# Last layer of a small conditioned transformer: first batch through all four experts first, grouped rows added to the result by indirect transfers

## The chip, the cores and the metric

The kernel runs on one core of a Trainium2 chip (trn2). The metric is device time in microseconds of one execution, median over runs. A profile is one further execution, recorded by the hardware profiler; its times are counted from the start of its span.

## The reference

The input is `x` of shape (4, 512, 288), four batches of 512 tokens, and a condition vector for each batch. A rotation of a 64-dimensional subspace comes first, then three transformer layers (attention with 16 heads, then a multilayer perceptron, each with shift, scale and gate from the condition). Only the last layer's perceptron matters here. It is a mixture of four experts with the best two chosen for each token:

```python
xn = _modulate(_ln(x), sh_mlp, sc_mlp)
xf = xn.reshape(-1, C)
gate_logits = xf @ w_gate
topk_logits, topk_idx = jax.lax.top_k(gate_logits, TOP_K)      # TOP_K = 2
gates = jax.nn.softmax(topk_logits, axis=-1)
cw = jnp.sum(jax.nn.one_hot(topk_idx, NUM_EXPERTS) * gates[..., None], axis=1)
hmid = gelu(jnp.einsum('tc,ech->eth', xf, w1) + b1[:, None, :])   # C = 288, hidden 1152
eo = jnp.einsum('eth,ehc->etc', hmid, w2) + b2[:, None, :]
moe = jnp.einsum('te,etc->tc', cw, eo).reshape(B, N, C)
return x + g_mlp[:, None, :] * moe
```

## The kernel before

Everything is written out by hand over ticks. Each engine walks through the same list of ticks, `TICKS`, and does at each of them its share of the main loop and then its items of the agenda (`items`, `agenda`, with a lag per kind and engine in `LAG`). The engines are in order, and only semaphores hold them together: a tick is a place in each engine's program, not a time.

A perceptron pass (a window) takes 512 token rows through one expert: nine hidden tiles of 128, two ticks each, 18 ticks. At an even tick TensorE multiplies a hidden tile (`hidden`, seven matmuls in split precision), at an odd one the back product of the tile two before it (`back`, twelve matmuls). ScalarE applies the gelu (`gelu_tile`); VectorE splits its result in a high and a low half (`G`), two operations. Weights come in six pieces per pass (`load_piece` on the SP queue), ScalarE takes the high half and, in the last layer, VectorE the low half (kind `split`). At the end of a pass VectorE adds the bias from PSUM into `rowt` (`finish`, kind `fin`, at tick 4 of the next pass).

The last layer has 13 passes. Batch 0 goes through each expert with all its rows; the rows of batches 1 to 3 are grouped by expert, in nine tiles of 512 rows. The order before is: batch 0 by experts 0, 1, 2 (`FRONT = 3`), the nine grouped tiles, and batch 0 by expert 3. Beside the first three passes the grouping is made for each batch: norm (`stats2`, `mean2` with GpSimd's `norm`), transposes (`ln2`: ScalarE takes the high part, GpSimd the low part), gate matmul (`gate`), logits turned (`gturn`; VectorE's `choose`), power on GpSimd (`gexp`), places within each expert (`rank`), weights (`weigh`), and modulated rows (`mod`, into the buffers `XG`). GpSimd then writes the rows to their places in the DRAM tensor `tok_rows` (`scatter`: eight indirect transfers, one for each quarter of the tokens and each of the two experts; it waits until they have landed). `table` works out which expert and which rows each tile has, `slots` where each token's two results will stand.

For a grouped tile SP loads its rows (`xg`, `tile_load`), TensorE transposes them in three parts (`lng`) with ScalarE's high and GpSimd's low parts, and after the pass SP stores `rowt` to the DRAM tensor `exp_rows` (`store`). In the last pass GpSimd gathers each token's two results (24 indirect transfers, `gather`); VectorE weighs and adds them, multiplies by the batch's gate and adds to the residual `X` (`merge`), and SP writes the four batches of the output.

Of the kernel before, what the change touches and what calls it, by code (L numbers as in the profile page):

```python
# [46 lines left out]
FRONT = 3  # L47
# [4 lines left out]
CW = C + 64  # L52
FAR = 65536.0
PLACED = 16 * 8
CONSTS = 32
# [171 lines left out]
def expert_of(v):  # L227

    return v if v < FRONT else v - GROUPED


def grouped_window(l, v):

    out = [(4, "fin", l, v - 1, 0)] if v > 0 else []
    i = v - FRONT
    if v > 0 and tile_of(v - 1) is not None:
        out += [(5, "store", l, i - 1, 0)]
    if v == 0:
        out += leaving(l) + [(4, "modrow", l, 1, 0), (12, "mod", l, 1, 0)]
        out += [(14, "gate", l, 0, 0), (15, "gturn", l, 0, 0), (16, "gexp", l, 0, 0), (18, "weigh", l, 0, 0)]  # L240
        out += [(16, "gate", l, 1, 0), (18, "gturn", l, 1, 0), (20, "gexp", l, 1, 0), (21, "rank", l, 1, 0), (23, "weigh", l, 1, 0)]
        out += [(22, "scatter", l, 1, 0)]
    if v == 1:
        out += [(t // 2, "stats2", l, 2, t) for t in range(TT)] + [(2, "mean2", l, 2, 0), (0, "modrow", l, 2, 0)]
        out += [(8 + c, "ln2", l, 2, c) for c in range(3)] + [(8, "mod", l, 2, 0)]
        out += [(11, "gate", l, 2, 0), (13, "gturn", l, 2, 0), (15, "gexp", l, 2, 0), (16, "rank", l, 2, 0), (18, "weigh", l, 2, 0)]
        out += [(17, "scatter", l, 2, 0)]
        out += [(9 + t // 2, "stats2", l, 3, t) for t in range(TT)] + [(11, "mean2", l, 3, 0), (11, "modrow", l, 3, 0)]
        out += [(15 + c, "ln2", l, 3, c) for c in range(3)] + [(17, "mod", l, 3, 0)]
    if v == 2:  # L250
        out += [(0, "gate", l, 3, 0), (2, "gturn", l, 3, 0), (4, "gexp", l, 3, 0), (5, "rank", l, 3, 0), (7, "weigh", l, 3, 0)]
        out += [(6, "scatter", l, 3, 0), (6, "table", l, 0, 0), (10, "slots", l, 0, 0)]
    if v + 1 < WINDOWS[l]:
        first = PIECE["w1", l, v + 1, 0]
        loads = {0: (-2, -2, 4, 6, 9, 11), 1: (0, 1, 2, 8, 10, 12), 2: (-3, -2, -1, 8, 10, 11)}.get(v, (-3, -2, -1, 8, 10, 12))
        out += [(t, "load", l, first + q, 0) for q, t in enumerate(loads)]
        out += [(t, "split", l, first + q, 0) for q, t in enumerate((5, 7, 9, 12, 14, 16) if v > 0 else (1, 3, 7, 9, 12, 15))]
        out += [(9 if v > 0 else 16, "side", l, v + 1, 0)]
    if i == -1:
        out += [(12, "xg", l, 0, 0)] + [(15 + c, "lng", l, 0, c) for c in range(3)]  # L260
    if 0 <= i < GROUPED - 1:
        out += [(1, "xg", l, i + 1, 0)] + [(11 + 2 * c, "lng", l, i + 1, c) for c in range(3)]
# [75 lines left out]
def row_room(l, s, i):  # L338
# [12 lines left out]
                gturn=0, weigh=0, rank=0, table=0, slots=0, merge=0, mod=0, split=1),  # L351
    "POOL": dict(gexp=0, setup=0, scatter=0, gather=0, mean1=1, mean2=1, ln1=1, ln2=1, lng=1, qk=1, out=1, proj=1, tok=1, root=3, split=1, centre=1, fin=1, wg=1,
                 ones=0, vones=0),
    "SP": dict(onerow=0, qk=2, max=1, place=0, load=0, wp=0, agate=0, mlpc=0, b2=0,
               modrow=0, xg=0, store=0, side=0),
# [32 lines left out]
def build(nc, a, out):  # L388
    with ExitStack() as ctx:  # L389
# [11 lines left out]
        tok_rows = nc.dram_tensor("tok_rows", (XROWS, CW), F32).ap()  # L401
        exp_rows = nc.dram_tensor("exp_rows", (GROUPED * N, C), F32).ap()
# [24 lines left out]

        XG = [at(o_qk + 43776 + 5632 * z, f"XG{z}", [128, TT, CW]) for z in range(2)]
        modr = at(o_qk + 43776 + 11264, "modr", [128, 2, CW])

        GA = [[XG[r][:, :, 0:C] for r in range(2)]]
        GA += [[at(o + 4608 * r, f"GA{o}{r}", [128, TT, C])[:, :, :] for r in range(2)] for o in (o_qk, o_qk + 23040)]

# [28 lines left out]
        X = rest("X", [128, B * TT, C])  # L462
        ident = rest("ident", [128, 128])
# [7 lines left out]
        euler = rest("euler", [128, TT, 4])  # L471
        xn = rest("xn", [128, TT, C + 64])
# [26 lines left out]
        cw = at(o_squares + 544, "cw", [128, B, TT, 4])  # L499
        idx = at(o_squares + 800, "idx", [128, SEL, TT, 2], U32)  # L500
        yidx = at(o_squares + 896, "yidx", [128, SEL, TT, 2], U32)
        cws = at(o_squares + 992, "cws", [128, SEL, TT, 2])
# [13 lines left out]
        moved = rest("moved", [128, 4])  # L516
# [5 lines left out]

        slot_a, slot_b = (rowt[:, k, 0:4 * SEL * TT].rearrange("p (n e) -> p n e", e=4) for k in range(2))
        slot_lohi = rowt[:, 2, 0:2 * SEL * TT].rearrange("p (n r) -> p n r", r=2)
# [176 lines left out]
        slots_ready = sem("slots_ready")  # L701
        yg_in = [sem(f"yg_in{j}") for j in range(SEL)]
        merged = sem("merged")
# [75 lines left out]
        def _(sp):  # L779
# [72 lines left out]
            for l in range(LAYERS):  # L852
# [6 lines left out]
            sp.dma_start(tok_rows.rearrange("(k p) c -> p k c", p=128),  # L859
                         act32[:, 0, 0:CW].unsqueeze(1).broadcast_to([128, XROWS // 128, CW])).then_inc(zero_out, 16)  # L860
# [11 lines left out]
            sp.wait_ge(zero_out, 16)  # L872
# [111 lines left out]
            for todo in agenda("SP"):  # L984
                for kind, l, i, k in todo:
# [14 lines left out]
                    elif kind == "store":  # L1000
                        tile_store(l, i)
# [4 lines left out]
            for b in (1, 0, 2, 3):  # L1006
                if b > 0:
                    sp.wait_ge(merged, b)
                else:
                    sp.wait_ge(out_ready, TT)  # L1010
                sp.dma_start(out[b].rearrange("(t p) c -> p t c", p=128), X[:, TT * b:TT * b + TT, :]).then_inc(out_done, 16)
            sp.wait_ge(out_done, 16 * B)

        @block.gpsimd
        def _(pool):
# [92 lines left out]
            def work(kind, l, i, k):  # L1108
# [79 lines left out]
                elif kind == "scatter":  # L1188

                    pool.wait_ge(zero_out, 16)  # L1190
                    pool.wait_ge(mod_done, i)
                    pool.wait_ge(idx_ready, i)
                    for t in range(TT):
# [4 lines left out]
                elif kind == "gather":  # L1198
                    if i == 0:
                        pool.wait_ge(ys_out, 16 * GROUPED)  # L1200
                        pool.wait_ge(slots_ready, 1)
                        pool.wait_ge(misc_full, MISC["lng", l, GROUPED - 1, 2] + 1)

                        pool.wait_ge(acc_full, TT * (WBASE[l] + FRONT + GROUPED))
                    for t in range(TT):
                        for r in range(2):
                            pool.indirect_dma_start(GA[i][r][:, t, :], None, exp_rows,
                                                    bass.IndirectOffsetOnAxis(yidx[:, i, t, r:r + 1], 0)).then_inc(yg_in[i], 16)
                    if i == SEL - 1:
                        for j in range(SEL):  # L1210
                            pool.wait_ge(yg_in[j], 16 * 2 * TT)
# [31 lines left out]
        def _(dve):  # L1243
# [138 lines left out]
            def finish(l, v):  # L1382
# [7 lines left out]
                if l == LAST and v > FRONT:  # L1390
                    dve.wait_ge(ys_out, 16 * min(v - FRONT, GROUPED))
# [3 lines left out]
                if l < LAST or tile_of(v) is not None:  # L1395
# [6 lines left out]
                for t in range(TT):  # L1402
                    ins = dve.scalar_tensor_tensor(out=X[:, TT * b + t, :], in0=rowt[:, t, :], scalar=cw[:, b, t, e:e + 1],  # L1403
# [8 lines left out]
            def merge(j, part):  # L1412

                first, second = GA[j]
                if part == 0:
                    dve.wait_ge(yg_in[j], 16 * 2 * TT)
                    for t in range(TT):
                        dve.tensor_scalar(first[:, t, :], first[:, t, :], cws[:, j, t, 0:1], None, ALU.mult).then_inc(dve_done, 1)  # L1418
                        step()
                    dve.wait_ge(dve_done, steps[0])  # L1420
                    for t in range(TT):
                        dve.scalar_tensor_tensor(out=first[:, t, :], in0=second[:, t, :], scalar=cws[:, j, t, 1:2],  # L1422
                                                 in1=first[:, t, :], op0=ALU.mult, op1=ALU.add).then_inc(dve_done, 1)
                        step()
                    return
                xb = X[:, TT * (j + 1):TT * (j + 2), :]
                dve.wait_ge(dve_done, steps[0])
                dve.wait_ge(mlp_in, mlp_in_total(LAST))
# [995 lines left out]
```

## Time and profile before

| | us |
|---|---|
| median of 3 runs | 1889.64 |
| lowest, highest | 1887.38, 1892.05 |
| the profiled execution, its own time | 1903.3 |
| its span | 1901.6 |

TensorE is busy for 88% of the span (1682.3 us), VectorE for 63%, ScalarE for 51%, GpSimd for 33%. The mean granted TensorE clock is 0.935 of full speed. The profile's page has for each engine its busy time, its share of the span and its number of instructions; then the span in 40 slices, the transfers, the chain that ended last and the costliest groups of instructions. The last layer's perceptron begins around 1398 us.

### The profile page before, as it was taken

How to read it: one execution, taken by the hardware profiler on the slowest of the kernel's cores; microseconds unless marked ns; L12 is line 12 of the kernel's file. 1: busy time of each engine (PE TensorE's matmuls, PEld its weight loads, DVE VectorE, ACT ScalarE, POOL GpSimd, SP SyncE). 2: the span in 40 equal slices, each digit the busy share in tenths (PEclk: the TensorE clock that was granted, in tenths of full speed). 3: DMA queues.
4: the chain of work that ended last, by engine and by line, in shares of the span. 5: the costliest groups of instructions: out<-in, count | busy, mean ns of one | idle time of the engine just before them, and what ended most of it. 6: DMA issues, size and time to landing. Idle time of an engine off the chain costs nothing. (4 is left out here: it accounts for less than half of the span.)

```text
span 1901.6 us, 27789 instructions
## 1 busy us (share of the span) xinstructions
PE 1682.3 (88%) x9395; PEld 1075.8 (57%) x9395; DVE 1196.0 (63%) x2624; ACT 978.7 (51%) x1720; POOL 629.8 (33%) x641
## 2 busy tenths in 40 slices
PE   6776899989998989899899999999898679999993
PEld 2443444433796634344369764444356469999992
DVE  7863677763565767677436567777548376656555
ACT  2323476657354466676655337676664235454530
POOL 4432122214554423341445332231435431111113
PEclk9999799989998879899889989999889799999996
DMA  7712333231001322313200213323223144544423
GB/s 247 246 61 65 103 103 93 93 108 48 11 1 42 101 72 70 92 55 114 70 20 1 88 54 102 101 91 98 72 70 118 65 127 125 156 138 155 140 82 106
DMA packets 104381, 175.98 MB, mean 93 GB/s; under 512 B 13675, under 2 KB 58659, under 8 KB 103951
## 3 DMA queue, kind: packets, MB, share of 16 engines
q1 hardware_dynamic: 101552, 166.33, 28.4%
q0 software_dynamic: 2688, 7.87, 1.3%
q8 instruction: 76, 1.25, 0.3%
q14 instruction: 65, 0.53, 0.1%
HBM read 122.48 MB, written 51.19 MB: 91 GB/s over the span
## 5 line engine op out<-in xcount | busy, mean ns | idle before, releaser
L1379 DVE TENSOR_REDUCE negmax<-ps 128x1 f32<-128x512 f32 x768 | 487.9, 680 | 233.1 <-PE ps L2152 229.7
L1978 ACT ACTIVATE Pr<-ps 128x512 f32<-128x512 f32 x768 | 410.9, 602 | 221.0 <-PE ps L2170 220.7
L1991 ACT ACTIVATE g<-ps,b1col 128x512 f32<-128x512 f32 x189 | 129.8, 688 | 301.9 <-PE ps L2131 247.9
L2170 PE MATMUL ps<-QK 55*128 55x512 f32 x768 | 240.5, 518 | 37.4 <-ACT Pr L1978 26.4
L2216 PE MATMUL ps<-W2a,G 128*128 128x288 f32 x1620 | 246.7, 302 | 13.0 <-issue 10.0
L2216 PEld LDWEIGHTS ps<-W2a,G 128*128 128x128 f32 x1620 | 231.6, 191 | 27.4 <-issue 13.7
L2184 PE MATMUL ps<-Pr,V 128*32 128x512 f32 x1536 | 224.9, 660 | 0.0
L2152 PE MATMUL ps<-QK 54*128 54x512 f32 x768 | 195.9, 445 | 23.6 <-DVE negmax L1379 7.9
L2170 PEld LDWEIGHTS ps<-QK 55*128 55x128 f32 x768 | 92.5, 193 | 204.6 <-ACT Pr L1978 106.9
L1733 DVE CAST G<-g 128x512 fp32r<-128x512 f32 x189 | 103.0, 545 | 157.3 <-ACT g L1991 152.2
L1134 POOL TENSOR_TENSOR HQ<-act,HQ 128x512 fp32r<-128x512 f32 (+1 forms) x69 | 91.6, 1327 | 254.3 <-ACT HQ L1953 120.1
L1735 DVE TENSOR_TENSOR G<-g,G 128x512 fp32r<-128x512 f32 x189 | 149.1, 789 | 6.5
L1134 POOL TENSOR_TENSOR stage<-act,stage 126x512 fp32r<-126x512 f32 (+1 forms) x60 | 77.4, 1289 | 205.7 <-ACT stage L1970 168.1
L2131 PE MATMUL ps<-HQ,W1a 128*128 128x512 f32 x441 | 121.5, 416 | 11.0 <-ACT g L1991 11.0
L2294 PE MATMUL ps<-WP,oT 128*128 128x288 f32 x384 | 126.3, 461 | 2.3 <-DVE oT L1650 2.2
L2152 PEld LDWEIGHTS ps<-QK 54*128 54x128 f32 x768 | 95.8, 199 | 49.2 <-DVE negmax L1379 23.0
L2294 PEld LDWEIGHTS ps<-WP,oT 128*128 128x128 f32 x384 | 72.8, 207 | 69.5 <-issue 35.6
L2131 PE MATMUL ps<-WQ,HQ 128*128 128x288 f32 (+1 forms) x560 | 99.2, 319 | 8.0 <-ACT stage L1970 3.3
L2131 PEld LDWEIGHTS ps<-WQ,HQ 128*128 128x128 f32 (+1 forms) x560 | 81.4, 198 | 43.2 <-issue 14.6
L2131 PE MATMUL ps<-HQ,W1b 128*128 128x512 f32 (+1 forms) x378 | 100.1, 404 | 2.7 <-POOL HQ L1134 2.7
L1139 POOL TENSOR_TENSOR oTok<-oTok,rsum 128x512 f32<-128x512 f32 x48 | 51.2, 1066 | 152.5 <-DVE rsum L1644 151.5
L2131 PEld LDWEIGHTS ps<-HQ,W1a 128*128 128x128 f32 x441 | 82.4, 196 | 31.7 <-ACT g L1991 14.4
(285 smaller groups left out, 2462.8 us busy)
## 6 DMA issues: line engine op xcount, KB each, us to landing
QK<-heads_t SPq DMA_DIRECT2D x192, 144.0 KB
heads_t<-stage SPq DMA_DIRECT2D x96, 252.0 KB
raw<-in_w SPq DMA_DIRECT2D x30, 576.0 KB
raw<-in_w SPq DMA_DIRECT2D x34, 432.0 KB
QK<-heads_t SPq DMA_DIRECT2D x192, 72.0 KB
tok_rows<-act SPq DMA_DIRECT2D x1, 10560.0 KB, 34.4
XG<-tok_rows SPq DMA_DIRECT2D x9, 704.0 KB, 4.3
WA<-in_ada_w SPq DMA_DIRECT2D x3, 1728.0 KB
```

Source lines behind the costliest of these rows:

```text
L1134: pool.tensor_tensor(lo, act32[rows, h % 2, :], hi.bitcast(F32), ALU.subtract).then_inc(low_done, 1)
L1379: dve.tensor_reduce(negmax[:, m % 2, h, t:t + 1], ps[:, row_bank(l, s, i), :], AX, ALU.max, negate=True).then_inc(a_free, 1)
L1733: dve.tensor_copy(G[:, n % 3, 0, :], g32[:, n % 2, :]).then_inc(g_hi, 1)
L1735: dve.tensor_tensor(G[:, n % 3, 1, :], g32[:, n % 2, :], G[:, n % 3, 0, :].bitcast(F32), ALU.subtract).then_inc(g_lo, 1)
L1978: act.activation(Pr[:, t % 2, 2 * half + pair, :], ps[:, (16 * s + u) % 3, :], ACT.Exp, scale=SCALE).then_inc(b_free, 1)
L1991: act.activation(g32[:, n % 2, :], ps[:, hidden_bank(s), :], ACT.Gelu if l == 1 else ACT.Gelu_apprx_tanh, bias=b1col[:, v % 4 if l == LAST ...
L2131: ins = mm(o, lhs(w, h, rows[w]), rhs(w, h, rows[w]), start=p == 0, stop=p == 6)
L2152: mm(ps[:, row_bank(l, s, i), :], QK[r:r + QROW, g, 0, pair, 128 * t:128 * t + 128], QK[r:r + QROW, g, 1, pair, :], start=True, stop=True) ...
L2170: mm(ps[:, k % 3, :], QK[r:r + QROW + 1, g, 1, pair, 128 * t:128 * t + 128], QK[r:r + QROW + 1, g, 0, pair, :], start=True, stop=True).the ...
L2184: ins = mm(ps[32 * i:32 * i + 32, 6, :], V[:, s // 4 % 2, t, c:c + 32], Pr[:, t % 2, i, :], start=t == 0, stop=t == TT - 1)
L2216: ins = mm(ps[:, t, 0:C], G[:, n % 3, x, 128 * t:128 * t + 128], W2[w_ % 2][:, w, ft, :], start=ft == 0 and p == 0, stop=ft == FT - 1 and ...
L2294: ins = mm(bank[:, 0:C], oT[:, (STEPS * l + 4 * i + g) % 5, 128 * k:128 * k + 128], WP[:, g, :], start=g == 0, stop=g == 3)
```

## The change

Batch 0 goes through all four experts first (`FRONT = 4`); the nine grouped tiles come behind. The grouping is spread over the first three passes and one load into the fourth, with later ticks for most items. The last pass is a grouped tile.

A row in `tok_rows` becomes longer by eight values (`PAY = CW + 8`): its four expert weights (written by `weigh`), three values that mark its batch (written by `mod`), and its row number in the output. Rows never written hold zero weights and the number of a row of batch 0, laid down when the buffer is filled at the start, in four transfers now.

For each grouped tile VectorE reads these values (`extras`, kind `ext`): the row numbers as integers, the weight of the tile's expert, and weight times batch mark. It makes from them the tile's gate, four times one product and two multiply-adds (`gates`, kind `gsum`), and after the pass it multiplies `rowt` by it into one of two buffers. GpSimd adds these rows to the output in DRAM by four indirect transfers with addition (`yadd`, at tick 4 of the next pass), and waits until they have landed. The output rows of batches 1 to 3 without the perceptron's part, and later batch 0's, are written beforehand (`init`). Stores to `exp_rows`, `slots`, `gather` and `merge` go.

```diff
-FRONT = 3
+FRONT = EXPERTS[-1]
+PAY = CW + 8
@@ def grouped_window(l, v): @@
-        out += [(5, "store", l, i - 1, 0)]
+        out += [(4, "yadd", l, i - 1, 0)]
     if v == 0:
-        out += leaving(l) + [(4, "modrow", l, 1, 0), (12, "mod", l, 1, 0)]
...
+        out += leaving(l)
+        for b, gate, turn, power, place, weight, move in ((0, 14, 15, 16, None, 18, None), (1, 17, 19, 21, 22, 23, 30),
+                                                          (2, 30, 32, 35, 35, 37, 42), (3, 43, 45, 47, 48, 50, 51)):
+            out += [(gate, "gate", l, b, 0), (turn, "gturn", l, b, 0), (power, "gexp", l, b, 0), (weight, "weigh", l, b, 0)]
+            if b > 0:
+                out += [(place, "rank", l, b, 0), (move, "scatter", l, b, 0)]
+        out += [(4, "modrow", l, 1, 0), (12, "mod", l, 1, 0), (18, "modrow", l, 2, 0), (29, "mod", l, 2, 0),
+                (31, "modrow", l, 3, 0), (38, "mod", l, 3, 0), (50, "table", l, 0, 0)]
+        out += [(16 + t // 2, "stats2", l, 2, t) for t in range(TT)] + [(18, "mean2", l, 2, 0)]
+        out += [(24 + 2 * c, "ln2", l, 2, c) for c in range(3)]
+        out += [(26 + t // 2, "stats2", l, 3, t) for t in range(TT)] + [(28, "mean2", l, 3, 0)]
+        out += [(36 + 2 * c, "ln2", l, 3, c) for c in range(3)]
+        out += [(17, "init", l, b, 0) for b in range(1, B)]
...
-        out += [(12, "xg", l, 0, 0)] + [(15 + c, "lng", l, 0, c) for c in range(3)]
+        out += [(4, "xg", l, 0, 0), (14, "ext", l, 0, 0)] + [(11 + 2 * c, "lng", l, 0, c) for c in range(3)]
+    if i == 0:
+        out += [(6, "init", l, 0, 0)]
...
+    if i >= 0:
+        out += [(6 + 2 * t, "gsum", l, i, t) for t in range(TT)]
     if v == WINDOWS[l] - 1:
-        out += [(6, "gather", l, j, 0) for j in range(SEL)]
-        out += [(t, "merge", l, j, part) for j, t in ((0, 16), (1, 20), (2, 21)) for part in range(2)]
-        out += [(21, "fin", l, v, 0)]
+        out += [(21, "fin", l, v, 0), (21, "yadd", l, i, 0)]
@@ gpsimd @@
+                elif kind == "yadd":
...
+                    pool.wait_ge(ext_ready, i + 1)
                     for t in range(TT):
+                        pool.wait_ge(res_ready, TT * i + t + 1)
+                        pool.indirect_dma_start(out_rows, bass.IndirectOffsetOnAxis(ids[:, i % 2, t:t + 1], 0),
+                                                res[i % 2][:, t, :], None, compute_op=ALU.add).then_inc(ys_out, 16)
+                    pool.wait_ge(ys_out, 16 * TT * (i + 1))
@@ vector, finish @@
+                if l == LAST and v >= FRONT:
+                    i = v - FRONT
+                    if i >= 2:
+                        dve.wait_ge(ys_out, 16 * TT * (i - 1))
+                    for t in range(TT):
+                        dve.wait_ge(acc_free, TT * U + t + 1)
+                        dve.tensor_tensor(res[i % 2][:, t, :], rowt[:, t, :], gsum[:, t, :], ALU.mult).then_inc(res_ready, 1)
+                    return
@@ vector @@
+            def gates(l, i, t):
...
+                dve.tensor_scalar(gsum[:, t, :], gbc[:, 1, :], wgt[:, i % 2, t, 0:1], None, ALU.mult).then_inc(dve_done, 1)
                 dve.wait_ge(dve_done, step())
+                for j in range(1, SEL):
+                    dve.scalar_tensor_tensor(out=gsum[:, t, :], in0=gbc[:, j + 1, :], scalar=wgt[:, i % 2, t, j:j + 1],
+                                             in1=gsum[:, t, :], op0=ALU.mult, op1=ALU.add).then_inc(dve_done, 1)
+                    dve.wait_ge(dve_done, step())
```

## Rows read from the trace of the kernel before

**Rows 1.** Windows: length, busy us (x instructions) of each engine, granted clock, DMA share.

```profile
1441.44:1497.66 56.22, 42.68 (x229) 35.55 (x227) 36.85 (x124) 24.47 (x36) 27.41 (x23) 0.85 0.35 109
1497.66:1560.04 62.38, 39.22 (x208) 31.82 (x205) 37.95 (x113) 16.97 (x24) 26.36 (x22) 0.86 0.36 115
1560.04:1590.54 30.50, 30.50 (x184) 27.68 (x184) 19.23 (x30) 14.94 (x21) 4.40 (x3) 1.00 0.37 102
1620.98:1651.42 30.44, 30.44 (x186) 27.62 (x185) 18.45 (x28) 15.07 (x22) 4.41 (x3) 1.00 0.48 144
1832.70:1881.80 49.10, 37.90 (x197) 33.35 (x195) 22.50 (x44) 6.30 (x10) 24.99 (x24) 0.84 0.34 97
```

**Rows 2.** Chain that ended last: start us, us, what.

```profile
1563.55 1.63 PE ps L2131 x7
1565.17 1.59 PE ps L2216 x12
...
1583.38 0.44 PE ps L2256 x4
```

**Rows 3.** Timeline, early passes: start us, us, instruction, idle before it and releaser.

```profile
1453.80 1.23 POOL L1195 DMA_INDIRECT tok_rows<-XG,idx  x1 [0.73 <-POOL shift L1102]
...
1470.86 4.26 POOL L1134 TENSOR_TENSOR HQ<-act,HQ 128x512 fp32r<-128x512 f32 x3 [3.81 <-DMA tok_rows<-XG,idx]
...
1475.19 0.12 PEld L2131 LDWEIGHTS ps<-HQ,Wg 128*4 128x4 f32 x2 [8.94 <-issue]
...
1498.01 1.59 POOL L1195 DMA_INDIRECT tok_rows<-XG,idx  x1 [0.29 <-POOL HMv L1134]
...
1511.14 1.25 POOL L1134 TENSOR_TENSOR HMv<-act,HMv 32x512 fp32r<-32x512 f32 x1 [1.62 <-DMA tok_rows<-XG,idx]
1512.46 0.12 PEld L2131 LDWEIGHTS ps<-HMv,Wg 128*4 128x4 f32 x2 [13.37 <-issue]
```

**Rows 4.** Timeline, last pass and end.

```profile
1862.32 0.69 ACT L1991 ACTIVATE g<-ps,b1col 128x512 f32<-128x512 f32 x1 [7.67 <-remote]
...
1876.57 0.69 ACT L1991 ACTIVATE g<-ps,b1col 128x512 f32<-128x512 f32 x1 [13.56 <-remote]
...
1893.12 1.81 DVE L1403 SCALAR_TENSOR_TENSOR X<-rowt,cw,X 128x288 f32<-128x288 f32 x4
```

**Rows 5.** Groups of VectorE in two grouped passes: busy us, mean ns, idle before.

```profile
L1735 DVE TENSOR_TENSOR G<-g,G 128x512 fp32r<-128x512 f32 x18 | 12.5, 692 | 0.6
L1733 DVE CAST G<-g 128x512 fp32r<-128x512 f32 x18 | 7.6, 424 | 10.2 <-ACT g L1991 10.2
```

**Rows 6.** Timeline, early passes: finish, modulation, power.

```profile
1452.61 1.54 DVE L1394 TENSOR_TENSOR rowt<-ps,agate 128x288 f32<-128x288 f32 x4
...
1455.59 1.80 DVE L1403 SCALAR_TENSOR_TENSOR X<-rowt,cw,X 128x288 f32<-128x288 f32 x4
...
1462.93 1.62 DVE L1465 TENSOR_TENSOR XG<-xn,modr 128x1408 f32<-128x1408 f32 x1
...
1464.59 1.62 DVE L1467 TENSOR_TENSOR XG<-XG,modr 128x1408 f32<-128x1408 f32 x1
...
1484.17 2.95 POOL L1215 TENSOR_TENSOR tmp<-euler,tmp 128x16 f32<-128x16 f32 x1 [7.00 <-DVE tmp L1550]
```

**Rows 7.** Page, DMA issues: count, KB, median us to landing.

```profile
XG<-tok_rows SPq DMA_DIRECT2D x9, 704.0 KB, 4.3
```

**Rows 8.** Groups of VectorE in the last 50 us.

```profile
L1422 DVE SCALAR_TENSOR_TENSOR GA<-GA,cws,GA 128x288 f32<-128x288 f32 x8 | 3.6, 511 | 0.1
...
L1418 DVE TENSOR_SCALAR GA<-GA,cws 128x288 f32<-128x288 f32 x8 | 2.4, 366 | 0.0
```

**Rows 9.** Gather line: duration ns min/median/max, first and last start.

```profile
L1207 POOL DMA_INDIRECT GA<-exp_rows,yidx x16: 947/950/1951, 1855.5 to 1876.1; - x16
```

**Rows 10.** Timeline, first grouped pass: GpSimd's first low part.

```profile
1581.51 1.28 POOL L1134 TENSOR_TENSOR HMv<-act,HMv 128x512 fp32r<-128x512 f32 x1 [21.53 <-ACT HMv L1944]
```

**Rows 11.** Page, DMA queues: packets, MB, share of 16 engines.

```profile
q8 instruction: 76, 1.25, 0.3%
```

More of the change, by code:

```diff
@@ L52 @@
 CW = C + 64
+PAY = CW + 8
 FAR = 65536.0
 PLACED = 16 * 8
-CONSTS = 32
+CONSTS = 35
 LEAD = 3
@@ L243, in grouped_window @@
[L243 to L249, printed above, removed]
@@ L425, in build @@
         HMq = at(o_qk + 16384, "HMq", [128, 5, N], F32R)
[L428 to L432, printed above, removed]
+        XG = [at(o_qk + 43776 + 5760 * z, f"XG{z}", [128, TT, PAY]) for z in range(2)]
+        modr = at(o_qk + 43776 + 11520, "modr", [128, 2, CW])
         def hq(b):
@@ L462, in build @@
         X = rest("X", [128, B * TT, C])
+        gsum = X[:, TT:2 * TT, :]
+        res = [X[:, TT * (2 + z):TT * (3 + z), :] for z in range(2)]
         ident = rest("ident", [128, 128])
@@ L700, in build @@
         ys_out = sem("ys_out")
-        slots_ready = sem("slots_ready")
-        yg_in = [sem(f"yg_in{j}") for j in range(SEL)]
-        merged = sem("merged")
+        pay_ready = sem("pay_ready")
+        ext_ready = sem("ext_ready")
+        res_ready = sem("res_ready")
+        init_out = sem("init_out")
         out_ready = sem("out_ready")
@@ L1410, in finish, with extras @@
                 dve.wait_ge(dve_done, steps[0])
[L1412 to L1419, printed above, removed]
-                    dve.wait_ge(dve_done, steps[0])
[L1421 to L1428, printed above, removed]
-                dve.tensor_tensor(first, first, bc3(gbc[:, j + 1, :], TT), ALU.mult).then_inc(dve_done, 1)
+            def extras(l, i):
+                side = XG[i % 2][:, :, CW:PAY]
+                dve.wait_ge(xg_in[i % 2], 16 * (i // 2 + 1))
+                if i >= 2:
+                    dve.wait_ge(ys_out, 16 * TT * (i - 1))
+                dve.tensor_copy(ids[:, i % 2, :], side[:, :, 7]).then_inc(dve_done, 1)
+                step()
+                weight = side[:, :, 0]
+                if i > 0:
+                    dve.tensor_scalar(mine[:, :], tidx[:, 0:4], where[:, 0, i - 1:i], 1.0, ALU.subtract, ALU.is_equal).then_inc(dve_done, 1)
+                    dve.wait_ge(dve_done, step())
+                    dve.tensor_tensor(seen[:, 0], side[:, :, 0:4], bc3(mine[:, :], TT), ALU.mult).then_inc(dve_done, 1)
+                    dve.wait_ge(dve_done, step())
+                    dve.tensor_reduce(cwt[:, :], seen[:, 0], AX, ALU.add).then_inc(dve_done, 1)
+                    dve.wait_ge(dve_done, step())
+                    weight = cwt[:, :]
+                dve.tensor_tensor(wgt[:, i % 2], side[:, :, 4:7], weight.unsqueeze(2).broadcast_to([128, TT, SEL]),
+                                  ALU.mult).then_inc(dve_done, 1)
+                dve.wait_ge(dve_done, step())
+                dve.sem_inc(ext_ready, 1)
@@ L1718, in work @@
                     table()
-                elif kind == "slots":
-                    slots()
-                elif kind == "merge":
-                    merge(i, k)
+                elif kind == "ext":
+                    extras(l, i)
+                elif kind == "gsum":
+                    gates(l, i, k)
                 else:
```

157 lines of the change are left out of this document (65 added, 92 removed).

## The prediction

> **What bounds the kernel now.** I read the views from the outside in. The page's slices say where TensorE isn't full: it is at nine tenths almost everywhere, and dips twice in the last layer, around 1450 to 1560 us and at the very end. The windows view, cut at the first hidden matmul of each expert pass, gives those dips a size [rows 1]. A grouped pass takes 30.44 us and TensorE is busy in all of it. The passes of batch 0's second and third expert take 56.22 and 62.38 us, and the last pass (batch 0's fourth expert) 49.10 us. The chain gives what a pass needs: 1.63 us for seven hidden matmuls and 1.59 to 1.63 us for twelve back matmuls, 3.22 us per hidden tile, so 9 x 3.22 = 29.0 us, and three sets of transposes of 0.44 us where the next rows are prepared, 30.3 us [rows 2]. So the two early passes stand about 60 us above their matmuls (less some 10 us of gate, transpose and rank matmuls), and the last one 20 us.
>
> The timeline says why. In the early passes GpSimd issues the eight scatters of a batch and then waits until they have landed; the low parts of the next batch's transposed rows are queued behind that, and the gate matmul waits for them: scatter of batch 1 from 1453.80 us, next GpSimd work at 1470.86 us, TensorE idle 8.94 us; scatter of batch 2 from 1498.01 us, next work at 1511.14 us, idle 13.37 us [rows 3]. After each gap the granted clock of the stretch is 0.85 or 0.86 instead of 1.00 [rows 1]: part of the matmuls run at the 1.2 GHz level. In the last pass ScalarE's gelus stand still for 7.67 and 13.56 us, released by something the profile can't name, exactly while the 24 gathers run [rows 4]; with them TensorE stops. Behind the last matmul, at 1881.8 us, come two merges, the bias, gate and weight of the last pass, and the output's transfer: 19.8 us to the end of the span at 1901.6 us.
>
> **The change, part by part, against the profiled span of 1901.6 us.** That execution took 1903.3 us, 13.7 us above the median of 1889.64 us; I assume the difference isn't in the last layer and subtract the same gain from the median.
>
> (1) TensorE's work stays the same: thirteen passes, the same gates and transposes. Up to 1441.44 us, the first matmul of the second pass, both kernels do nearly the same. Then come three passes of batch 0 instead of two and one grouped tile: 3 x 29.0 = 87.0 us, nine transposes of 0.44 us = 4.0 us, and two gates, three turns and three ranks of logits, which I put at 9 us: 100 us. An upper bound is TensorE's busy time in the three stretches they replace, 42.68 + 39.22 + 30.50 = 112.4 us, which holds matmuls at the lower clock [rows 1]. After them eight grouped passes of 30.44 us and one of 29.0 us: 272.5 us. Without a stall the last matmul would end at 1441.4 + 100 + 272.5 = 1813.9 us, 67.9 us earlier.
>
> (2) Stalls that go: scatters now stand behind the low parts of the next batch in GpSimd's queue (scatter of batch 1 at tick 30, low parts at 25 to 29; batch 2 at 42, low parts at 37 to 41), so the 8.94 and 13.37 us go, and with them the low clock. The gathers go, with the 20 us above the matmuls in the last pass.
>
> (3) Stalls that come. VectorE works 36.85 + 37.95 + 19.23 = 94.0 us in the three stretches [rows 1]; without the slot computation (about 2 us) and the statistics that move ahead (2 us), with the extra columns (1.4 us), it is 91 us of 100. It is in order, and it may run late by about 4 us: the two halves of a tile (0.42 + 0.69 us [rows 5]) are done 3.7 us after its hidden matmuls start and used 8.1 us after. Adding its items pair of ticks by pair of ticks, it passes that in three places. At tick 22 the finish of the first pass (1452.61 to 1457.4 us, 4.8 us [rows 6]), rank and weights stand together: 1 us of stall. At tick 29 the modulation (two of 1.62 us, and three small new ones, 3.75 us): 2 us. At tick 37 the weights of batch 2 wait for the power on GpSimd (2.95 us), and that is queued behind the scatter of batch 1: eight issues and a landing took 13.1 to 17.1 us [rows 3], so VectorE stands 3 to 6 us, then meets modulation and finish: 4 us of stall, bounds 2 and 8. The tile's first rows are loaded once the third scatter has landed: by the same prices at about tick 63, with 4.3 us for the load [rows 7] just when its transposes come: 1 us, bounds 0 and 6.
>
> (4) Grouped passes. VectorE's 18.45 us of 30.44 [rows 1] gains twelve gate operations (per quarter 0.37 + 2 x 0.51 us and three waits, 1.5 us; 6.0 us [rows 8]), four products (0.45 us each at most) and the extras (seven small ones, 1.4 us): 27.5 us. The pairs of ticks 4 to 14 carry 3.7 to 4.3 us against TensorE's 3.22 to 3.66: it falls behind by 3 us, under the 4 us it may, and catches up at 16 to 2. No stall in the middle; I take 4 us in all nine passes (the first has the long finish too), bounds 0 and 20.
>
> (5) The indirect adds: four per pass on GpSimd, at tick 4. No row shows an accumulating transfer. Nearest rows: a gather's issue 0.95 us and 0.30 us to the next [rows 9]; a landing 1.62 or 3.81 us [rows 3]. So 6.6 to 8.8 us for four and their wait, starting about 10 us into a pass. GpSimd then has nothing until the next rows' low parts, 21.5 us into it, and idles 21.53 us before them [rows 10]: hidden. Those low parts may come 4.8 us later before the next pass waits (ScalarE's third copy needs the first low part), so four adds are free up to 16 us, 4.1 us each. Below, the cost is nothing; above, see the rival.
>
> The Trainium skill bears on that wait: "DMA: Bandwidth & Descriptors", section Rules for kernel authors, says that an accumulating transfer reads its destination and writes it later, with nothing holding the bytes between, so that the next must wait for its semaphore. That makes the wait in GpSimd's queue part of the price and no slack to be optimised away; no run here shows the read's own time.
>
> (6) The end. The last bias adds overlap TensorE's last quarter (0.6 us behind it), first product 0.45 us, four adds 5.0 us, landing 3 us, end 0.5 us: 10 us, bounds 9 and 20, instead of 19.8 us. Output rows of batches 1 to 3 (1.7 MB) leave at tick 17 and of batch 0 in the fifth pass; the stretches there have a DMA share of 0.35 and 0.48 [rows 1]: hidden.
>
> (7) The opening: filling the row buffer in four transfers and 1.6 us more of GpSimd constants. The columns use GpSimd's first root about three columns later: nothing.
>
> Sum: 1813.9 + 8 (windows two to four) + 4 + 10 = 1835.9 us, a gain of 65.7 us. On the median: 1889.6 - 65.7 = 1824 us. With every low bound 1816, with every high bound short of a rival 1859; the range goes lower because the 13.7 us between the profiled execution and the median have no place yet.
>
> **Rivals.** (a) VectorE becomes the bound of the grouped passes. For it: 27.5 of 30.4 us, and its operations stretch beside GpSimd's. Against: the slack above. From 10% longer new operations and conversions on, passes of 32.5 us: 8 x 2.1 = 17 us, and 4 us more early: 1845 us. (b) The unnamed stall travels with indirect transfers. 24 gathers went with 21.2 us of standing ScalarE [rows 4]: 0.88 us each, times 36 adds 32 us: 1856 us. Against it: the 24 scatters show none. The Trainium skill, "Runtime: NRT & Kernel Launch", section Instruction fetch mechanics, has each engine fetch its instructions in 16 KiB blocks over a DMA queue of its own; the page's instruction queue with 76 packets and 1.25 MB [rows 11] agrees in size, and if that fetch is what was late, adds between weight loads could hold it too. (c) Slower: accumulating transfers that read, add and write row by row take long, and GpSimd's wait holds the next pass's low parts. Free up to 4.1 us each; each further us costs 4 us in eight passes and 4 at the end, 36 us: from 5.9 us each the gain is gone; at 7 us the time is about 1929 us. Only the distance from the rows (1.7 to 2.2 us each with the wait) speaks against. (d) The regrouping doesn't do what it says: GpSimd, late behind norm and power, lets a scatter stand in front of a gate again, 9 to 13 us twice: 1846 us.
>
> **How the numbers follow.** The forecast 0.64 (own range 1808 to 1842), (a) 0.13, (b) 0.08, (c) 0.09, (d) 0.06. From 1806 to 1857 the range holds the forecast, (a), (d) and most of (b). Runs of this kernel differ by 0.25%, so 0.3% (5.7 us) is about what can be told from no change. Faster: all but (c), and a fifth of (c): 0.91; same 0.02; slower 0.07.
>
> **What would show it.** No gap above 3 us between gates and clock 1.00 in the second to fourth pass; first grouped matmul near 1550 us; grouped passes of 30.4 to 31 us, VectorE at nine tenths; no gap of ScalarE in the last pass; 10 us behind the last matmul. Wrong, if GpSimd's low parts of the next tile start after 26 us in a pass, or VectorE's halves end every hidden tile's wait.

## The result

| | before | changed kernel |
|---|---|---|
| median | 1888.51 us (4 runs, 1883.37 to 1892.05) | 1844.63 us (4 runs, 1836.84 to 1845.99) |
| ratio, 95% interval | | 0.9761 [0.9725, 0.9797] |
| profiled execution, span | 1903.3, 1901.6 | 1845.99, 1844.3 |

The change saves 43.9 us; 65.7 were forecast (1824 us; the range, 1806 to 1857, holds the time). A third of the forecast gain did not come.

The windows view of the changed kernel, cut at the first hidden matmul of each pass (columns as in [rows 1]: length, then busy us of TensorE, its weight loads, VectorE, ScalarE and GpSimd, then the clock). Passes two, three and four, the first two grouped passes, one from the middle, and the last up to its last matmul:

```profile
1426.13:1465.58 39.45, 35.65 (x216) 30.70 (x214) 36.33 (x117) 21.85 (x33) 17.60 (x17) 1.00 0.40 117
1465.58:1514.00 48.42, 36.50 (x207) 31.67 (x206) 34.94 (x101) 16.33 (x22) 26.57 (x19) 0.86 0.36 116
1514.00:1546.39 32.39, 30.68 (x185) 27.51 (x184) 25.61 (x45) 15.04 (x22) 11.76 (x10) 1.00 0.56 174
1546.39:1579.05 32.66, 30.99 (x186) 27.47 (x184) 28.99 (x48) 15.16 (x22) 4.34 (x3) 1.00 0.40 127
1579.05:1609.48 30.43, 30.43 (x186) 27.56 (x184) 28.04 (x50) 14.94 (x21) 10.85 (x7) 1.00 0.55 141
1671.19:1702.05 30.86, 30.68 (x185) 27.49 (x184) 28.50 (x50) 15.05 (x22) 11.03 (x7) 1.00 0.55 145
1794.59:1827.53 32.94, 32.75 (x197) 29.35 (x195) 23.21 (x47) 6.30 (x10) 6.45 (x4) 1.00 0.16 19
```

From the second pass's first matmul (1441.44 us before, 1426.13 after) to the span's end it is 460.2 us before and 1844.3 - 1426.13 = 418.2 us after: 42.0 us less, where the forecast had 1835.9 - 1441.4 = 394.5. (The spans differ by 57.3 us; the other 15.3 us lie before the second pass, and the experiments below put them down to chance.) With [rows 1], the 42.0 us are 28.8 us in the three passes from the second on (149.1 us, now 120.3), 16.2 us in the last pass (49.1, now 32.9) and 3.0 us behind it (19.8, now 16.8), less 6.0 us that the eight grouped passes in between take more (242.2, now 248.2). The missing 23.7 us lie in three places:

| | forecast | measured | difference |
|---|---|---|---|
| passes two to four | 100 + 8 | 39.45 + 48.42 + 32.39 = 120.3 | +12.3 |
| nine grouped passes to the last matmul | 272.5 + 4 | 1827.5 - 1546.4 = 281.1 | +4.6 |
| last matmul to the end | 10 | 1844.3 - 1827.5 = 16.8 | +6.8 |

Of the passes two to four, the third has the only slow clock (0.86) and the only large gap. Its timeline, with the instructions of three engines around the gap:

```profile
1470.47 0.96 POOL L1209 DMA_INDIRECT tok_rows<-XG,idx  x1 [0.30 <-issue]
...
1474.84 2.93 POOL L1226 TENSOR_TENSOR tmp<-euler,tmp 128x16 f32<-128x16 f32 x1 [3.40 <-DMA tok_rows<-XG,idx]
...
1477.80 0.17 DVE L1600 TENSOR_TENSOR tmp<-tmp,chosen 128x16 f32<-128x16 f32 x1 [7.73 <-POOL tmp L1226]
1477.85 2.87 POOL L1147 TENSOR_TENSOR HMv<-act,HMv 128x512 fp32r<-128x512 f32 x2
...
1479.63 1.63 DVE L1740 TENSOR_TENSOR G<-g,G 128x512 fp32r<-128x512 f32 x1
1481.19 1.61 DVE L1495 TENSOR_TENSOR XG<-xn,modr 128x1408 f32<-128x1408 f32 x1
...
1483.07 1.62 DVE L1503 TENSOR_TENSOR XG<-XG,modr 128x1408 f32<-128x1408 f32 x1
1484.61 1.49 DVE L1738 CAST G<-g 128x512 fp32r<-128x512 f32 x1
...
1486.13 0.69 DVE L1740 TENSOR_TENSOR G<-g,G 128x512 fp32r<-128x512 f32 x1
1486.75 1.54 DVE L1403 TENSOR_TENSOR rowt<-ps,agate 128x288 f32<-128x288 f32 x4
...
1487.34 2.98 PE L2221 MATMUL ps<-W2a,G 128*128 128x288 f32 x11 [11.30 <-DVE rowt L1403]
```

Read it backwards. TensorE stands for 11.30 us until the bias adds (L1403) free its accumulator; they stand behind the halves of two hidden tiles (G, four operations), the modulation of batch 3 (L1495, L1503) and the weights of batch 2 (L1600) on VectorE; those wait 7.73 us for the power on GpSimd (L1226); and that stands behind the landing of scatter 1 (L1209).

The grouped passes are close to [rows 1]'s 30.44 us, with VectorE at 28.5 us instead of 18.5. The end, on the timeline:

```profile
1826.49 1.55 DVE L1403 TENSOR_TENSOR rowt<-ps,agate 128x288 f32<-128x288 f32 x4 [1.85 <-PE ps L2221]
1827.96 1.55 DVE L1410 TENSOR_TENSOR X<-rowt,X 128x288 f32<-128x288 f32 x4
1829.20 1.74 POOL L1220 DMA_INDIRECT out<-X,ids  x1 [17.23 <-DVE X L1410]
1831.24 1.55 POOL L1220 DMA_INDIRECT out<-X,ids  x1 [0.30 <-issue]
1833.09 1.55 POOL L1220 DMA_INDIRECT out<-X,ids  x1 [0.30 <-issue]
1834.95 1.55 POOL L1220 DMA_INDIRECT out<-X,ids  x1 [0.30 <-issue]
```

All adds, by the source view of their line (duration ns min, median, max), and who waited for them:

```profile
L1220 POOL DMA_INDIRECT out<-X,ids x36: 1543/1688/2023, 1588.6 to 1834.9; - x36
...
who waited for it (us, times):
  POOL HQ L1147: 16.3, 4
  POOL HMv L1147: 12.9, 3
```

### The profile page after: what moved, and what is told of

It is laid out like the page before. It is cut to its first block, busy times and chain, and to the rows that moved or that the text cites. A ratio compares the mean times of both kernels' runs of the same rounds, so it can differ in the third digit from the quotient of the medians.

```text
span 1844.3 us, 27973 instructions
## 1 busy us (share of the span) xinstructions
PE 1665.0 (90%) x9395; PEld 1065.5 (58%) x9395; DVE 1271.2 (69%) x2776; ACT 977.1 (53%) x1720; POOL 666.9 (36%) x656
## 3 DMA queue, kind: packets, MB, share of 16 engines
q0 software_dynamic: 6720, 9.74, 2.8%
q8 instruction: 76, 1.25, 0.3%
## 4 chain that ended last, share of the span: by engine, by line
PE 56%; DVE 19%; issue 7%; ACT 7%; DMA 4%; POOL 4%; SPq 2%; DVEq 0%; ACTq 0%; POOLq 0%
PE ps L2136 17%; PE ps L2189 8%; PE ps L2221 8%; PE ps L2175 8%; PE ps L2299 6%; PE ps L2157 5%; ACT Pr L1983 2%; DMA heads_t<-stage 2%; DVE G L1738 2%; DVE X L1460 2%; PE ps L2275 2%; DVE negmax L1390 1%; DVE G L1740 1%; DVE W1a L1715 1%; DVE GT L1316 1%
## 5 line engine op out<-in xcount | busy, mean ns | idle before, releaser
L2157 PE MATMUL ps<-QK 54*128 54x512 f32 x768 | 198.0, 447 | 18.5 <-DVE negmax L1390 8.2
L2136 PE MATMUL ps<-HQ,W1a 128*128 128x512 f32 (+1 forms) x693 | 185.2, 407 | 6.7 <-ACT g L1996 6.7
L1738 DVE CAST G<-g 128x512 fp32r<-128x512 f32 x189 | 106.8, 565 | 102.3 <-ACT g L1996 100.8
L1740 DVE TENSOR_TENSOR G<-g,G 128x512 fp32r<-128x512 f32 x189 | 154.8, 819 | 6.5
L2136 PEld LDWEIGHTS ps<-HQ,W1a 128*128 128x128 f32 (+1 forms) x693 | 126.8, 192 | 35.2 <-ACT g L1996 9.9
L2136 PEld LDWEIGHTS ps<-WQ,HQ 128*128 128x128 f32 (+1 forms) x560 | 80.5, 196 | 42.0 <-issue 13.7
L1220 POOL DMA_INDIRECT out<-X,ids x36 | 61.8, 1717 | 110.6 <-DVE X L1410 102.4
```

The lines of the kernel that those rows point to most:

```text
L1738: dve.tensor_copy(G[:, n % 3, 0, :], g32[:, n % 2, :]).then_inc(g_hi, 1)
L1740: dve.tensor_tensor(G[:, n % 3, 1, :], g32[:, n % 2, :], G[:, n % 3, 0, :].bitcast(F32), ALU.subtract).then_inc(g_lo, 1)
L2136: ins = mm(o, lhs(w, h, rows[w]), rhs(w, h, rows[w]), start=p == 0, stop=p == 6)
L2157: mm(ps[:, row_bank(l, s, i), :], QK[r:r + QROW, g, 0, pair, 128 * t:128 * t + 128], QK[r:r + QROW, g, 1, pair, :], start=True, stop=True) ...
```

## The experiments

Ratios are to the kernel before, run beside each. "The stretch" is the time from the second pass's first matmul to the span's end in the profiled execution.

**Both kernels again.** 

> The changed kernel again, nothing edited: the partner of the runs beside it. All theories: 1837 to 1846 us, ratio to the kernel before 0.973 to 0.980.

Measured: 1847.67 us, ratio 0.9749 [0.9708, 0.979]; stretch 1850.4 - 1432.92 = 417.5 us, passes two to four 119.7 us, gap 10.15 us. Stretch and passes repeat within 1 us, the gap within 1.2; the median is 1.7 us above the range that I had given for it.

> The kernel before again, nothing edited, to see how far its stretches repeat. If they repeat as those of the changed kernel do: from the second pass to the end of the span 460 us, last pass 49 us. If the stalls beside the gathers vary (44.0 us for that pass where the scatters were late): 454 to 457 us, and with it a part of the 13.7 us by which the profiled execution stood above its median.

Measured: 1891.18 us; stretch 1889.5 - 1433.34 = 456.2 us, last pass to its last matmul 45.52 us instead of 49.10. The second case: of the 42.0 us some 4 were chance of the first profile, and the change is worth 38 to 43 us in the stretch. Up to the second pass, the five profiles of kernels made from the one before took 1420 to 1441 us (mean 1429.6), nine of those made from the changed one 1420 to 1435 (mean 1427.8): the opening and the earlier layers neither gain nor lose what this can tell, and the first profile was 12 us above its mean there. That and these 4 us are more than the 13.7 us that had no place.

**The gap in the third pass.**

```diff
-(2, 30, 32, 35, 35, 37, 42)        # weigh of batch 2
+(2, 30, 32, 35, 35, 41, 42)
```

> Only the weights of batch 2 move, from tick 37 to tick 41, behind the finish. Theory (VectorE stands at them for the power on GpSimd, which stands behind the landing of scatter 1; the bias adds of tick 40 are what TensorE waits for): VectorE's wait of 7.7 us goes, TensorE's stall of 11.3 us falls to 4 or less with the slow clock behind it, 8 to 11 us less than the changed kernel. Rival (VectorE has too much work there, modulation of batch 3 and finish, whatever it waits for): 3 us less or nothing, and a stall of 8 us or more stays in front of the first back product of the fourth pass.

Measured: 1844.09 us, ratio 0.9728 [0.9692, 0.9764]; passes two to four 39.45 + 42.43 + 34.54 = 116.4 us, stretch 414.3 us, 3.2 to 3.9 us less (the medians differ by 3.6 us, which is inside their noise). The gap is 4.82 us. VectorE, freed from the power, ran into another wait (timeline):

```profile
1479.46 1.66 DVE L1495 TENSOR_TENSOR XG<-xn,modr 128x1408 f32<-128x1408 f32 x1 [2.52 <-DMA tok_rows<-XG,idx]
...
1482.93 1.49 DVE L1738 CAST G<-g 128x512 fp32r<-128x512 f32 x1
1484.45 1.64 DVE L1740 TENSOR_TENSOR G<-g,G 128x512 fp32r<-128x512 f32 x1
1486.01 1.54 DVE L1403 TENSOR_TENSOR rowt<-ps,agate 128x288 f32<-128x288 f32 x4
```

The modulation of batch 3 writes the buffer that scatter 1 still reads. Theory and rival each had half: the power's wait was real, and behind it stood the same landing a second time.

```diff
-(38, "mod", l, 3, 0)
+(47, "mod", l, 3, 0)               # and weigh of batch 2 at 41
```

> As the run beside it, and the modulation of batch 3 from tick 38 to tick 47. Theory: another 2 to 3 us less than with the weights moved alone, 10 to 13 us less than the changed kernel. Rival (the wait moved from the weights to another instruction that follows the power): no more than 3 us less than the changed kernel.

Measured: 1834.96 us, ratio 0.9696 [0.9658, 0.9733], 12.7 us under the changed kernel on the same chip. Passes two to four 40.44 + 38.02 + 32.23 = 110.7 us, stretch 408.7 us, 9 us less; no gap in front of the bias adds of the third pass. The windows of the second and third pass:

```profile
1423.54:1463.98 40.44, 36.97 (x215) 31.69 (x214) 37.28 (x119) 21.86 (x33) 18.59 (x17) 0.96 0.39 120
1463.98:1502.00 38.02, 35.81 (x206) 31.16 (x206) 34.39 (x101) 16.21 (x22) 25.73 (x19) 0.96 0.45 143
```

VectorE does the same work (34.4 us against 34.9): it was the order around one landing, not the load. I had called this VectorE's 4 us of lateness.

**The order alone, in the kernel before.**

```diff
-(22, "scatter", l, 1, 0)   -(17, "scatter", l, 2, 0)
+(29, "scatter", l, 1, 0)   +(19, "scatter", l, 2, 0)
```

> The kernel before, with the scatter of batch 1 moved from tick 22 to 29 and that of batch 2 from tick 17 to 19 of the next pass, behind the low parts of the next batch's rows. Theory (the gaps come from the order in GpSimd's queue, but the third pass is needed to have room: norm, power and modulation of batch 3 then stand behind the scatters): the gaps before the two gates go, others come, the two passes together 0 to 8 us shorter than 118.6. Rival (order alone was enough, the fourth expert's pass at the front adds nothing here): the two passes 18 to 22 us shorter, and a ratio to the kernel before of about 0.99.

Measured: 1872.11 us, ratio 0.9932 [0.9909, 0.9955], stretch 443.0 us. Windows of its second and third pass:

```profile
1428.76:1483.59 54.83, 41.12 (x229) 33.91 (x227) 37.93 (x123) 24.10 (x36) 26.67 (x23) 0.88 0.37 112
1483.59:1532.84 49.25, 38.39 (x208) 32.16 (x205) 39.66 (x113) 17.30 (x25) 29.27 (x22) 0.92 0.46 146
```

104.1 us instead of 118.6, and 2.5 us given back in the pass behind. The gaps in front of the gates shrink to 3.0 and 2.8 us, but the first comes back, 8.5 us long, in front of the transposes of batch 3, whose norm now stands behind the scatter (timeline):

```profile
1476.08 1.09 PE L2270 MATMUL ps<-ident,xn 128*128 128x128 f32 x4 [8.46 <-ACT xn L1859]
```

Neither forecast of mine: the order is worth 13 us alone, nearly a third of the change. That the rest of those gaps needs the room of another pass is argued from this row; no run shows it by itself.

**The gathers of the kernel before.** First taken out with the merges, then replaced by plain transfers of 128 fixed rows:

```diff
-pool.indirect_dma_start(GA[i][r][:, t, :], None, exp_rows,
-                        bass.IndirectOffsetOnAxis(yidx[:, i, t, r:r + 1], 0)).then_inc(yg_in[i], 16)
+n = 128 * ((8 * i + 2 * t + r) % (GROUPED * TT))
+pool.dma_start(GA[i][r][:, t, :], exp_rows[n:n + 128, :]).then_inc(yg_in[i], 16)
```

> The kernel before without the gathers and without the merges: the output rows of batches 1 to 3 lack the perceptron's part. Theory (ScalarE's unnamed stalls of 7.7 and 13.6 us come with the gathers): the stalls go, the last pass takes 29 to 30 us instead of 49.1, and with the merges gone 3 to 5 us less behind it, 22 to 25 us less than the kernel before. Rival (the stalls belong to that place, the last pass itself): the last pass stays above 45 us and only the merges' part goes, 5 us less.

> The kernel before with its 24 gathers as plain transfers of 128 rows each, issued by GpSimd at the same place; the rows are not those of the tokens. Theory (it is the indirect transfers that ScalarE and TensorE stand beside, by the fetch of instructions or otherwise): no unnamed stall of ScalarE, last pass 32 us or less. Rival (24 transfers of GpSimd of this size in a row do it, of whatever kind): stalls of 5 us or more stay, last pass 40 us or more.

Measured: without them 1862.75 us, ratio 0.9894 [0.9859, 0.993], some 20 us less than before; stretch 433.3 us. With plain transfers 1871.74 us in one run. The last pass to its last matmul, in the windows of the kernel without gathers and of the one with plain transfers:

```profile
1814.80:1847.31 32.51, 32.50 (x197) 29.44 (x195) 14.68 (x28) 6.30 (x10) 0.00 (x0) 1.00 0.11 37
```

```profile
1813.63:1850.23 36.60, 34.15 (x197) 30.73 (x195) 22.52 (x44) 6.30 (x10) 13.11 (x24) 0.95 0.41 130
```

The floor of that pass is 32.5 us, not 29.0: it holds two more back products than the distance between two passes. With the indirect gathers it took 49.1, 45.5 and 44.0 us in three profiles. With plain transfers it took 36.6 us: ScalarE shows no unnamed wait, and TensorE waits once, 2.45 us, for a G that stands behind a merge on VectorE. The long stalls come with the indirect form in this place, as the theory had it, at 7.4 to 12.5 us; 4.1 us of the pass's length came with plain gathers and merges, and the 32 us that the theory gave for it did not hold. It is one run, and two things changed along with the form: GpSimd issued sixteen plain transfers in 8.64 us, where an indirect one takes 0.95 us and 0.30 us to the next [rows 9], and the plain ones read neighbouring rows. Pace and rows were not tested by themselves.

**The price of the addition.**

```diff
-res[i % 2][:, t, :], None, compute_op=ALU.add).then_inc(ys_out, 16)
+res[i % 2][:, t, :], None).then_inc(ys_out, 16)
```

> The 36 last transfers write their rows without adding: the output rows lack what was in them before. Theory (the addition is the price: the descriptors take longer to make and the landing holds a read): issue 1.0 us each instead of 1.7, landing 2 to 4 us instead of 4 to 7, the stretch behind the last matmul 11 to 12 us instead of 16.8, in all 5 to 6 us less. Rival (any indirect write of these rows takes so long): issue 1.5 us or more, 0 to 2 us less.

Measured: 1838.76 us, ratio 0.973 [0.9683, 0.9777], which can't be told from the changed kernel's; its trace can. Passes are 30.84 us, 30.86 in the changed kernel, and behind the last matmul it takes 1836.6 - 1823.1 = 13.5 us instead of 16.8. Source view and end of its timeline:

```profile
L1220 POOL DMA_INDIRECT out<-X,ids x36: 959/1160/2157, 1584.4 to 1828.8; - x36
```

```profile
1824.82 1.14 POOL L1220 DMA_INDIRECT out<-X,ids  x1 [19.51 <-DVE X L1410]
1826.26 0.96 POOL L1220 DMA_INDIRECT out<-X,ids  x1 [0.30 <-issue]
1827.52 0.96 POOL L1220 DMA_INDIRECT out<-X,ids  x1 [0.30 <-issue]
1828.79 0.96 POOL L1220 DMA_INDIRECT out<-X,ids  x1 [0.31 <-issue]
```

Issue: theory right at the end, 4.9 us for four instead of 7.3; in a middle pass the four take 7.3 us instead of 7.9, so little of it is saved there. Landing: theory wrong, 6.85 us from the last issue's end to the end of the span, with addition 7.8 (both with whatever else ends the execution). In the passes GpSimd's waits for the landing vanish from the view (16.3 + 12.9 us in the changed kernel), and no pass gets shorter: they were off the path, as forecast.

**How near VectorE is to the bound.** The twelve gate operations of a tile left out, and done twice, for tiles 1 to 8:

```diff
-out += [(6 + 2 * t, "gsum", l, i, t) for t in range(TT)]
+out += [(6 + 2 * t, "gsum", l, i, t) for t in range(TT if i == 0 else 0)]
```

```diff
+for _ in range(2 if i > 0 else 1):        # around the three operations of gates()
```

> The gates are made for the first grouped tile alone, the later tiles use the same: 96 of VectorE's 108 gate operations are left out. Theory (VectorE is nearly, not quite, the bound of the grouped passes): passes of 30.4 us instead of 30.86, about 3.5 us less in all. Rival a (VectorE is the bound): 1 us or more less in each of eight passes, 8 us or more. Another (the 0.4 us have nothing to do with it): no change.

> The twelve gate operations are done twice for tiles 1 to 8: 6.0 us more of VectorE in each of eight passes. Theory (VectorE has 27.5 us of work in 30.86, so it becomes the bound): passes of 33 to 34.5 us, 17 to 29 us more in all. Rival (VectorE waits a good deal and has more room than its sum shows): passes of 31 to 31.5 us, 2 to 5 us more.

Measured: 1842.72 us, ratio 0.9763 [0.9719, 0.9807], and 1887.2 us, ratio 0.998 [0.995, 1.001]. A middle pass of the first and of the second, in windows:

```profile
1647.70:1678.12 30.42, 30.42 (x185) 27.59 (x184) 22.53 (x38) 15.04 (x22) 11.86 (x7) 1.00 0.57 148
```

```profile
1694.96:1732.04 37.08, 33.55 (x186) 29.72 (x185) 34.26 (x63) 14.94 (x21) 12.18 (x7) 0.91 0.46 121
```

With 6.0 us less of VectorE a pass is 0.44 us shorter, as the theory had it; the 3.5 us in all can't be seen in the median. With 5.8 us more a pass is 6.2 us longer, above what either side had expected, and the whole gain is gone. Its granted clock is 0.91, and TensorE is busy for 33.55 us instead of 30.68, so a part of the 6.2 us may be the clock; the run doesn't separate the two. These passes fit VectorE's work plus some 2.4 to 2.8 us (28.50 + 2.36, 34.26 + 2.82), or TensorE's 30.42 us, whichever is more. By that the changed kernel stands just past the knee, at 28.5 us of VectorE; nothing between 28.5 and 34.3 us was run.

**Better versions.** Weights of batch 2 at 41, modulation of batch 3 at 49, `table` at 62, places and weights of batch 1 at 24 and 25, and in the last pass

```diff
+if l == LAST and v == WINDOWS[l] - 1:
+    for t in range(TT):
+        dve.tensor_tensor(rowt[:, t, :], ps[:, t, 0:C], b2_at(l, v), ALU.add)
+        dve.tensor_tensor(res[i % 2][:, t, :], rowt[:, t, :], gsum[:, t, :], ALU.mult)
```

> The changed kernel with VectorE's items spread: weights of batch 2 at tick 41, modulation of batch 3 at 49, the table at 62, places and weights of batch 1 at 24 and 25 behind the finish, and in the last pass each quarter's bias and product next to each other. Theory (each stall of passes two to four is VectorE late at a named item): passes two to four 104 to 108 us instead of 120, end behind the last matmul 15.7 us, in all 12 to 16 us less than the changed kernel. Rival (VectorE has no room in these passes, a stall only moves): no better than the run with weights and modulation moved, about 10 us less.

Measured: 1839.01 us, ratio 0.9764 [0.9736, 0.9792]; passes 43.59 + 37.54 + 30.80 = 111.9 us, stretch 408.7 us. Passes three and four are 2 us better than with two items moved, the second is 3 us worse (4 us above the changed kernel's 39.45): TensorE's transposes of batch 2 wait 2.98 us for VectorE to read the places from the bank they share (`place_in`). The end takes 15.6 us. By the median it is no gain, and the 104 to 108 us expected for the passes did not hold.

> As the spread version, but places and weights of batch 1 stay at ticks 22 and 23, where they were. Theory (the places must be read before the next transposes get their bank; that alone cost the second pass its 4 us): second pass 39.5 us, passes two to four together 107 to 109 us, from the second pass to the end of the span 404 to 406 us against 418 in the changed kernel, 1826 to 1834 us. Rival (chance decides between 109 and 112): no difference from the spread version, 408 us or more.

Measured: 1833.19 us, ratio 0.9717 [0.9668, 0.9766]; passes 39.45 + 38.06 + 31.53 = 109.0 us, end 15.7 us, stretch 1831.6 - 1425.57 = 406.0 us, 12.2 us under the changed kernel, as expected. By medians this and the run with two items moved (1834.96) can't be told apart; both beat the kernel before, and by their traces the changed kernel too, by 9 and 12 us.

## Why the time lay in the range and the gain was a third short

The steps in the prediction's order.

(1) TensorE's work: right. Without their stalls passes two to four are about 100.7 us (120.3 less 19.6: gaps of 1.83, 1.25, 0.72, 0.61, 11.30 and 1.71 us and 2.2 us of slow clock), for 100. But the last pass was put at 29.0 us: that is its distance to a next pass; up to the last matmul it has two back products more (32.5 us without stalls).

(2) The stalls that go: right. TensorE's matmuls have no gap in front of a gate, and ScalarE no unnamed wait in the last pass. (The 8.94 and 13.37 us of [rows 3] are the waits of the weight loads; the matmuls stood 8.74 and 12.95 us.) But the low clock (0.86) came back behind the one large gap of the third pass.

(3) The stalls that come: the step that failed most, 8 us for about 19.6 (17.4 of gaps, 2.2 of slow clock). Tick 22 had 1.83 us for my 1, the modulation of tick 29 gaps of 1.25 and 0.72 us behind it for my 2. At tick 37 I took 4 us, bounds 2 and 8; it was 11.3, and 2.2 of slow clock behind it. I had seen the wait for the power behind the scatter, and measured lateness by the G halves, to which I gave 4 us of slack. The bias adds that follow have less: VectorE waited 7.73 us and TensorE 11.30. Between the end of that wait and them stood 9 us of VectorE's work (1477.80 to 1486.75 us). And I missed that the modulation of batch 3 waits for the same landing, for its buffer (2.52 us once the other wait was gone). Two gaps had no term: 0.61 us for the read of the places, and 1.71 us in the fourth pass, behind the weights of batch 3 and the table. The first tile's load was on time.

(4) Grouped passes: right, 248.2 us for eight, 247.5 forecast. Of VectorE's terms the product was 0.45 us and a multiply-add 0.52, but its work came to 28.5 us, not 27.5: most of that is one small operation of the extras (L1446), 1.04 us instead of 0.17, held by GpSimd. Rival (a) was nearer than its time says: its mechanism is there, at 0.44 us a pass.

(5) The adds: hidden in the passes, as forecast, but dearer. In the middle pass from 1671.19 us four issues take 7.9 us, and GpSimd goes on 4.2 us behind them, when they have landed (timeline; the row behind is the first of the last listing below):

```profile
1681.23 1.74 POOL L1220 DMA_INDIRECT out<-X,ids  x1 [10.49 <-DVE X L1410]
...
1687.45 1.69 POOL L1220 DMA_INDIRECT out<-X,ids  x1 [0.31 <-issue]
```

That is 12.1 us, 3.0 each with the wait, where I had 1.7 to 2.2; under the 4.1 that I called free. The next rows' first low part starts 22.2 us into the pass, not 21.5, released by the landing; with the plain write it is 21.8 us. So the adds begin to push it, but a pass is no longer for it (30.86 us, 30.84 with the plain write). Rival (c) false.

(6) The end: 16.8 us for 10. The first add is issued 1.7 us behind the last matmul (1.05 forecast), the four take 7.3 us (5.0, priced by the gather's 0.95), landing and end 7.8 (3.5). The last price stood in my own rows: VectorE's last operation ended at 1893.12 + 1.81 = 1894.93 us [rows 4], and the span at 1901.6, 6.7 us for the output's landing and the end. I took a landing from the scatters' waits instead [rows 3].

(7) The opening: no cost that can be seen.

Rival (b) is false though its stall is real: 36 indirect adds, four at a time, show none of it, 24 indirect gathers in a row do. Rival (d) is false as stated; its core, GpSimd's landing wait in front of something needed, is what cost most, in another place: the power instead of the gate.

Of the signs that the prediction named, the clock of the third pass and the end failed. The first grouped matmul at 1546.39 us, near the 1550 forecast, is luck: the opening was 15.3 us shorter in this profile and passes two to four 12.3 us longer than forecast.

## What to carry to other kernels

When an engine waits in order for a transfer to land, list everything behind that wait on every engine, and everything that needs the transfer's buffer; here the one landing was met twice, and moving two items by 4 and 9 ticks gave 9 us in the trace. Lateness of an in-order engine is measured against the next thing another engine needs from it, not against the usual one. And a second engine at nine tenths of a pass can already be at its bound: here 5.8 us more of its work cost 6.2 us a pass.

## What the runs showed of the hardware

- An indirect transfer with addition takes GpSimd 1.54 to 2.02 us to issue (median 1.69), the same without 0.96 to 2.16 us (median 1.16); the software queue moved the same 9.74 MB in 6720 and in 3264 packets. From the end of the last issue to the end of the span it was 7.8 and 6.85 us.
- A row of 24 indirect gathers makes this pass 7.4 to 12.5 us longer (three profiles) than 24 plain transfers from GpSimd (one profile), with ScalarE standing 4.7 to 7.7 us once and 11.3 to 13.6 us once; the plain ones don't hold it, nor do 8 indirect scatters or 4 adds in a row. The instruction queue has 76 packets and 1.25 MB in each of these kernels, so its sum neither speaks for a late fetch nor against it. What holds ScalarE stays open.
- VectorE's operations stretch when they meet GpSimd's low parts: a G half of 0.69 us took 1.63 to 1.66 us, a conversion of 0.42 us 1.49, and each ended as if it had begun when the GpSimd operation ended (1693.35 + 1.46 + 0.69 = 1695.50 us, seen 1693.69 + 1.66 = 1695.35): it looks held, not slowed. It goes both ways: GpSimd's low part of 1.27 us took 2.30 us at 1483.52 us, beside VectorE's L1503, which ended at 1484.69 us. In a grouped pass (timeline of the changed kernel):

```profile
1693.35 1.46 POOL L1147 TENSOR_TENSOR HMv<-act,HMv 128x512 fp32r<-128x512 f32 x1 [4.20 <-DMA out<-X,ids]
1693.69 1.66 DVE L1740 TENSOR_TENSOR G<-g,G 128x512 fp32r<-128x512 f32 x1
...
1696.66 1.29 POOL L1147 TENSOR_TENSOR HMv<-act,HMv 128x512 fp32r<-128x512 f32 x1 [1.86 <-ACT HMv L1949]
1696.77 2.10 DVE L1715 TENSOR_TENSOR W2b<-raw,W2b 128x864 fp32r<-128x864 f32 x1
...
1700.32 1.27 POOL L1147 TENSOR_TENSOR HMv<-act,HMv 32x512 fp32r<-32x512 f32 x1 [2.37 <-ACT HMv L1949]
...
1700.59 1.04 DVE L1446 TENSOR_TENSOR wgt<-XG,cwt 128x12 f32<-128x12 f32 x1
```

  These three meetings cost VectorE 2.9 us a pass (1.66 for 0.69, 2.10 for 1.06, 1.04 for the 0.17 us that L1446 takes where it meets none), against the 0.44 us by which the pass is above TensorE's own. The Trainium skill, "SBUF — State Buffer", section Who interferes with whom, says that a VectorE instruction with two inputs in SBUF contends with a GpSimd instruction that reads SBUF; the three meetings above agree with that rule. The conversion, with one input, is not covered by it.
